# Square sums behind the first group of the output projection, and two of four sets of weight turns in front of the final projection, in a state-space loop on one Trainium2 core

## The reference

```python
fx = (x @ W_fx.T + b_fx)                     # 8 heads x 64
sw = softmax((xm @ W_slice.T + b_slice) / temp)   # per node and head: weights over 64 slices
st = einsum(fx, sw) / (sw.sum(nodes) + 1e-5) # 64 slice states per graph, 512 wide
z, xBC, dt = split(st @ in_w.T)              # input projection
x, B, C = split(silu(conv(xBC)))
y = scan both ways over the 64 states with decays exp(dt * -exp(A_log)) ...
yg = y * silu(z)
yg = yg * rsqrt(mean(yg ** 2, -1) + 1e-5) * norm_w
ot = yg @ out_w.T                            # output projection, 512 x 512
out = einsum(ot, sw)                         # slices back to nodes
return out @ out_w2.T + out_b                # final projection, 512 to 128
```

## Time and profile before

| | |
|---|---|
| median of 3 runs | 3788.64 us (3781.55 to 3794.27) |
| profiled execution, own time | 3786.41 us |
| its span in the profile | 3784.7 us |
| granted TensorE clock, mean | 0.874 of full |
| the loop's full turns, by the start of `squares` | 338.66 us (turn 0) to 1404.79 us (turn 13) |
| TensorE busy over the span | 3137.6 us, 83% |
| VectorE busy | 2418.1 us, 64% |
| ScalarE busy | 1339.5 us, 35% |

### The profile page before, as it was taken

One profiled execution on the slowest core, in us unless ns is written; L12 is line 12 of the kernel. 1 busy time (PEld: TensorE's weight loads), 2 busy tenths in 40 slices (PEclk: granted clock), 3 DMA queues, 4 the chain that ended last, 5 costly groups with the idle time before them and its releaser, 6 DMA issues. The chain is left out here.

```text
span 3784.7 us, 55514 instructions
## 1 busy us (share of the span) xinstructions
PE 3137.6 (83%) x21257; PEld 1981.2 (52%) x21257; DVE 2418.1 (64%) x4190; ACT 1339.5 (35%) x2535; POOL 235.8 (6%) x200
## 2 busy tenths in 40 slices
PE   6479999999999998444459997599876988986998
PEld 5245555555555554243326666366543656653665
DVE  6737777767777775598653345688993345763333
ACT  3233344334444443201334443212112434543444
POOL 0000000000000000000000000033220003420000
PEclk7689999999999999655679996699987987987999
DMA  3311112112111211100012311000001211102222
GB/s 39 96 51 38 38 38 57 41 38 51 37 38 43 55 38 35 54 1 1 29 52 72 77 45 16 5 0 0 1 0 43 67 39 44 43 15 66 70 69 69
DMA packets 145005, 152.56 MB, mean 40 GB/s; under 512 B 66628, under 2 KB 124896, under 8 KB 142328
## 3 DMA queue, kind: packets, MB, share of 16 engines
q1 hardware_dynamic: 144800, 149.72, 16.1%
HBM read 141.26 MB, written 8.44 MB: 40 GB/s over the span
## 5 line engine op out<-in xcount | busy, mean ns | idle before, releaser
L816 DVE TENSOR_TENSOR f_hg<-f_hs,f_gb 128x640 f32<-128x640 f32 x320 | 263.9, 826 | 507.5 <-ACT f_hs L798 448.0
L2306 PE MATMUL hy_ps<-hy_uT,hy_win 128*128 128x512 f32 x1152 | 498.7, 594 | 0.0
L798 ACT ACTIVATE f_hs<-f_ph,f_b1t 128x320 f32<-128x320 f32 x640 | 335.1, 527 | 405.7 <-PE f_ph L766 402.4
L766 PE MATMUL f_ph<-XNP,f_w 128*128 (+1 forms) x1280 | 404.5, 440 | 12.9 <-PEq L648 8.6
L781 PE MATMUL f_po<-f_hg,f_w 128*128 128x320 f32 x1280 | 404.6, 439 | 9.1 <-DVE f_hg L816 9.1
L2306 PEld LDWEIGHTS hy_ps<-hy_uT,hy_win 128*128 128x128 f32 x1152 | 217.8, 190 | 281.0 <-issue 281.0
L766 PEld LDWEIGHTS f_ph<-XNP,f_w 128*128 128x128 f32 x1280 | 247.4, 194 | 117.4 <-issue 18.8
L781 PEld LDWEIGHTS f_po<-f_hg,f_w 128*128 128x128 f32 x1280 | 240.5, 191 | 126.2 <-issue 20.9
L2366 PE MATMUL hy_ps<-hy_wo,hy_yg 128*128 128x512 f32 x512 | 257.6, 663 | 0.0
L1829 PE MATMUL er_c<-XNG 128*128 128x400 f32 x544 | 205.0, 517 | 21.7 <-POOL XNG L1760 21.5
L2366 PEld LDWEIGHTS hy_ps<-hy_wo,hy_yg 128*128 128x128 f32 x512 | 105.8, 212 | 130.2 <-issue 130.2
(11 more groups left out here) (525 smaller groups left out, 5512.7 us busy)
## 6 DMA issues: line engine op xcount, KB each, us to landing
f_gb<-gate_rows SPq DMA_DIRECT2D x32, 1280.0 KB, 8.3
XNG<-hy_decays SPq DMA_DIRECT2D x32, 1024.0 KB, 10.9
hy_rb<-hy_inverse SPq DMA_DIRECT2D x128, 128.0 KB, 3.1
f_gb<-gate_rows SPq DMA_DIRECT2D x16, 640.0 KB, 5.0
g_KB<-g_keys SPq DMA_DIRECT2D x32, 320.0 KB, 4.5
hy_xn<-XNP SPq DMA_DIRECT2D x1, 4096.0 KB, 14.1
hy_XC<-hy_xn SPq DMA_DIRECT2D x16, 256.0 KB
XNG<-in_L_ffn_edge_index_dram SPq DMA_DIRECT2D x2, 2048.0 KB
```

Of the source, the lines that this page charges most:

```text
L766: pe.matmul(psh[e % 2][k][:], w1[:, e, k * 128:(k + 1) * 128], chunk_view(g, c), start=True, stop=True).then_inc(h_ps, 1)
L798: ins = act.activation(hs[:, e % 2, k, :], psh[e % 2][k][:], ACT.Gelu, bias=b1t[:, e * H2 + k:e * H2 + k + 1])
L816: dve.tensor_tensor(hg[:, e % 2], hs[:, e % 2], gb[:, par, e, None, :].broadcast_to([128, H2, CH]), ALU.mult).then_inc(hg_ready, 1)
L2306: mm = pe.matmul(p[:], win[:, t, m * 128:(m + 1) * 128], uT[:, t, :], start=(t == 0), stop=(t == KT - 1))
```

## The change

Only TensorE's list is changed. Group 0 of the output projection goes in front of the square sums, with a wait for `yg1` (the gated rows) of its own. `transposed` is taken out of `slices` and becomes a function of the turn: sets 0 and 1 of chunk c + 2 are turned right behind `back_to_nodes(c)`, ahead of `dt_down` and the final projection, and sets 2 and 3 stay behind the slice states in the next turn. No instruction is added or dropped, and the other engines' lists are as they were.

```diff
+            def transposed(q):
+                for t in range(KT):
+                    mm = pe.transpose(PS[TURNED[q]][:, t * 128:(t + 1) * 128], sw[:, q, t * 128:(t + 1) * 128], g.ident[:])
+                mm.then_inc(s["sT_ps"], 1)
+
             def slices(k):
...
-                for q in range(CHP):
-                    if q == 1:
-                        settle(s["rn"], k + 1)
-                    elif q == 2:
-                        settle(s["f_out"], k + 1)
-                    elif q == 3:
-                        settle(s["sT_out"], 4 * k + 1)
-                    transposed(q)
+                settle(s["rn"], k + 1)
+                settle(s["f_out"], k + 1)
+                transposed(2)
+                settle(s["sT_out"], 4 * k + 1)
+                transposed(3)
...
             def output_projection(k, groups):
+                pe.wait_ge(s["yg1"], k + 1)
...
                 if there(c):
+                    output_projection(c, range(1))
                     squares(c)
-                    output_projection(c, range(CHP - 1))
+                    output_projection(c, range(1, CHP - 1))
                 if there(c + 2):
                     slice_sums(c + 2)
                 if there(c):
                     output_projection(c, range(CHP - 1, CHP))
                     back_to_nodes(c, par)
+                if there(c + 2):
+                    transposed(0)
+                    transposed(1)
```

## The result

The changed kernel takes 3762.45 us (median of 6 runs, 3757.22 to 3776.83), beside 3790.72 us for the kernel before on the same occasions: a ratio of 0.9935 over all runs of both, 95% interval 0.9915 to 0.9956, 17 to 32 us less. By this ratio 24.6 us were gained, by the two medians 28.3 us; forecast were 32.7 us. Measured once more on another occasion the ratio was 0.9941 (0.9922 to 0.996). The profiled execution is the slowest of the six, 3776.83 us with a span of 3775.1 us; its times are those of the one profile and not of the median.

What follows compares the result with a forecast made beforehand. TensorE was taken as the loop's bound, busy 1032.7 of 1066.19 us. Gains of 18.2, 2.4, 6.0 and 6.1 us, together 32.7, gave 3756 us; likeliest case 3744 to 3767 us, stated range 3744 to 3777.

Steps and rivals of the forecast that it cites:

- The squares' part: From gains to slice sums: group 0 ahead of the squares removes idle time and clock loss, less two waits; 1.15 us gained.
- The new waits: TensorE would wait 0.7 to 0.8 us at group 2 for ScalarE's copy, 0.9 us at the slice sums for VectorE.
- The table load: Between root and exponentials: by the profile row it costs 0.35 us a turn, by the skill page's drain 1.7 us.
- The turns' part: Moved weight turns, nodes to steps_down: 0.7 us gained behind uT, 0.55 lost at the final projection; 0.15 us a turn gained.
- If the clock still fell here, the waits would swallow it: At the squares and group 2: the two new waits about equal a fall's cost, so the slice sums' start would hardly move.
- rival 1: Clock falls elsewhere in most turns, ahead of steps_down, slice sums or input projection; up to 24 us, 3780 us; chance 0.14.
- Behind the wait and the square sums, the clock falls: In output groups 0 to 2 of the kernel before: clock drops to 0.50 after the squares, costing 1.7 us.
- The last two turns: Turns 14 and 15, gains or gated rows to nodes: 6.0 and 6.1 us gained from removed wait and clock loss.
- the half-clock stretch: Turn 15, after TensorE's long idle time: one slow stretch of 1.7 us left in, so 6.1 us gained instead of 7.8.
- The sum: Whole kernel: 18.2 us from turns 0 to 13, 2.4 from longer falls, 6.0 and 6.1 at the end; together 32.7 us.
- the term for turns 0 to 13: Loop turns 0 to 13: 14 x (1.15 + 0.15) = 18.2 us, plus 2.4 us for longer clock falls.

Runs made afterwards that it cites:

- e2: Only the moved weight turns (sets 0 and 1), square sums back ahead of group 0, against the kernel before: 3785.94 us beside 3793.43, ratio 0.9979.
- e3: The changed kernel with gains cut in two, groups 2 and 3 behind output group 0: 3759.08 us, ratio 0.9916 to the kernel before.
- e6: The changed kernel with gains in three pieces around output group 0 and the squares, the last with dt_down ahead of group 2: 3745.55 us, ratio 0.9877 to before.
- e1: Only output group 0 moved ahead of the square sums, all weight turns left in place, against the kernel before: 3764.2 us, ratio 0.9933.
- e0: The changed kernel measured again, nothing altered: 3767.66 us beside 3793.81 for the kernel before, ratio 0.9941.

## Why the prediction was right, and where it was not

**The squares' part, a turn without a fall: right.** From the end of gains (992.94) to the slice sums (1005.95) it is 13.0 us, beside 14.24 before: 1.23 us gained, forecast 1.15. The new waits were forecast at 0.7 to 0.8 and 0.9 us and are 0.61 and 0.84. The exponentials were delayed by 0.24 us in place of 0.35, as `root` started 0.98 us behind the squares and not 1.09.

**The table load: the row was right.** ScalarE's timeline of the changed kernel has the load exposed:

```profile
997.30 0.26 ACT L2489 ACTIVATE hy_rms<-hy_ps,eps 128x4 f32<-128x4 f32 x1 [9.35 <-PE hy_ps L2353]
997.58 1.28 ACT L2425 ACT_TABLE_LOAD   x1
998.88 1.91 ACT L2425 ACTIVATE hy_sw<-hy_sw 128x2048 f32<-128x2048 f32 x1
```

The exponentials follow it by 0.02 us. The drain that the Trainium skill gives on its page "ScalarE: Activation LUTs", section "What ACT_TABLE_LOAD costs", does not show here either.

**The turns' part: right.** The final projection starts 3.86 us behind the nodes (1011.97 to 1015.83) and not 3.17, 0.69 us later where 0.55 was forecast; the input projection starts 10.71 us behind them and not 11.48; from nodes to `steps_down` it is 48.57 us (931.57 to 980.14) and not 48.78, 0.2 us gained, forecast 0.15. The small miss hides two larger ones: `steps_down` starts 37.92 us behind `uT` (942.22 to 980.14) and not 38.15, so 0.9 us was gained there where 0.7 was forecast, against 0.69 lost where 0.55 was. Alone (e2) it changed hardly more than the measurement tells.

**"If the clock still fell here, the waits would swallow it": wrong, and this is the step that failed.** It was written for a fall behind the squares, and no run had one there after the change. I had looked for a fall in new places (rival 1) and had left out that the change moves group 0, at the start of which the clock can fall, from behind the squares to in front of them. There it delays squares, `root`, the table load and the exponentials, and with them both ends for which TensorE waits; the two waits keep their length. Ten falls at 1.7 us are 17 us in the first profile, five are 8.5 us in the second. The gap between the 32.7 us forecast and what was gained, 4.4 us by the medians and 8.1 us by the ratio, is of this order; the falls of the executions without a profile are not known. Rival 1 had the right price and a wrong place: none of the falls was ahead of `steps_down`, at the slice sums or behind the moved transposes. The Trainium skill's page "TensorE: Matmul & The Clock Gate", section "Part 4: PE-mode transpose", spoke for the last of these; no run here shows it, the clock stayed full there in every profile.

**"Behind the wait and the square sums, the clock falls": half right as a cause.** Without the wait it fell less often, and in each run in other turns. The kernel before had a turn that showed where to look, turn 10:

```profile
1157.00:1158.00 1.00, 0.07 (x1) 0.00 (x0) 0.93 (x2) 0.00 (x0) 0.00 (x0) 0.56 0.00 0
...
1158.21 1.87 PE L2356 MATMUL hy_ps<-mean_w,hy_uT 128*128 128x1 f32 x8 [1.15 <-DVE hy_uT L2629]
```

The clock was down at about 1157.1, as `gains` ended and 1.1 us ahead of the squares. With `gains` in two pieces (e3) or three (e6) it did not fall at all.

**The last two turns: undersized.** From nodes 13 to nodes 15 it took 122.93 us in place of 136.58, 13.7 us gained, forecast 12.1; the half-clock stretch that I left in turn 15 did not come. In the second profile it did (group 0 took 6.74 us), and the gain was 11.0 us.

**The sum.** The loop gave 16.4 us in the first profile and 23.5 in the second (nodes 15), forecast 32.7. Where the falls are taken out, in e3, it gave 30.1 us. The miss lies in the term for turns 0 to 13: 18.2 + 2.4 = 20.6 us were forecast, and the nodes of turn 13 came 2.8 us earlier in the first profile and 12.5 us in the second. The falls are 17 and 8.5 us of that, the four longer turns 1.4 us. So it is in part luck that the time lay within the range: had every turn kept its fall, as in the kernel before, 14 x 1.7 = 24 us would have been paid, the price of rival 1, and 3780 us lies outside. And the rest of the kernel, which the sum took as constant, varies by as much as the miss (last section).

## What to carry to other kernels

When a wait is moved or covered, look at what the covering work is in front of: a slow spell of it (here a clock fall) now delays everything that the covered step releases, and a wait that hangs on that step comes later with it and absorbs nothing. A new wait on another engine's chain is room for work that stands elsewhere on the critical way; filling it brought more here (e6 beside e3, both without falls: turns of 79.6 us in place of 80.5) than the change's second half (0.2 us a turn). Small products that stand together cost more than their own time in this kernel, since the full products behind them ran at half clock in many turns; with dense work between the pieces (e3, e6) they did not.

## What the runs showed of the hardware that was not expected

Two profiles of one program differ in how often the clock falls (10 and 5 of 14 turns), with the same instructions ahead of it: whether a stretch of 2.3 us of small products is followed by a fall is not decided by the program alone. The kernel before, whose sparse stretch of gains, wait and squares was longer, fell in every turn.

The part of the kernel behind the loop, which no edit touched, varies too. Its last graph layer (from the first to the last transpose of L1120) took, by windows of the kernel before, of the changed kernel and of e1:

```profile
3135.40:3383.30 247.90, 241.06 (x2635) 166.59 (x2636) 174.02 (x156) 125.22 (x279) 89.85 (x28) 0.85 0.14 36
```

```profile
3116.10:3371.20 255.10, 248.44 (x2636) 171.16 (x2636) 174.04 (x156) 125.54 (x279) 89.90 (x28) 0.82 0.14 35
```

```profile
3110.00:3353.40 243.40, 237.21 (x2635) 164.21 (x2636) 174.03 (x156) 125.23 (x279) 89.88 (x28) 0.87 0.14 37
```

VectorE, ScalarE and GpSimd are busy for the same time to 0.3 us; TensorE takes 237 to 248 us for the same products at granted clocks of 0.87 to 0.82. That is up to 12 us between executions from one untouched layer, as much as most of the edits here are worth. It is not the edit: the changed kernel, once more in e0, took 247.6 us for the same stretch (3108.00 to 3355.60), at a clock of 0.85. It is the larger part of why 16.4 us gained by the end of the loop were 9.6 us in the span of the changed kernel's profile, and the reason that the starts of the nodes told these kernels apart where the medians did not.
